# A two-layer graph network on one core: a tile's one-hots as three VectorE broadcasts, self weights copied by POOL, room and landing told in larger groups

## What is computed

```python
# layer 0
agg = segment_sum(h[src], dst, 12500)
z = (1 + eps_gin) * h + agg
z = relu(z @ W1 + b1) @ W2 + b2
z = (z - mean(z, 0)) * rsqrt(var(z, 0) + 1e-5) * gamma + beta
x1 = layernorm(x + (z + x))
# layer 1
support = segment_sum(edge_weight[:, None] * x1[dst], src, 12500)
out = layernorm(x1 + relu(support @ weight))
```

## Time and profile before

| | us |
|---|---|
| timed, median of 3 | 4,327.98 (4,326.99 to 4,332.28) |
| span of the profiled execution | 5,351.1 |
| busy PE / PE weight loads | 3,721.5 (70%) / 3,045.6 (57%) |
| busy POOL | 3,177.6 (59%) |
| busy DVE | 2,301.2 (43%) |
| busy ACT | 1,495.5 (28%) |

### The profile page before, as it was taken

One profiled execution on the slowest core, in us unless ns is written; L12 is line 12 of the kernel. 1 busy time (PEld: TensorE's weight loads), 2 busy tenths in 40 slices (PEclk: granted clock), 3 DMA queues, 4 the chain that ended last, 5 costly groups with the idle time before them and its releaser, 6 DMA issues.

```text
span 5351.1 us, 79415 instructions
## 1 busy us (share of the span) xinstructions
PE 3721.5 (70%) x16131; PEld 3045.6 (57%) x16132; DVE 2301.2 (43%) x5448; ACT 1495.5 (28%) x4377; POOL 3177.6 (59%) x3352
## 2 busy tenths in 40 slices
PE   2677676667667776767742667777777777777777
PEld 2565555555555655656632556566665666665666
DVE  2545454545555544545563233333333333333333
ACT  2444444445444444444552000000000000000001
POOL 6666655565656665666335666666666666666662
PEclk6887888888887878888855789888888888888898
DMA  4333333333333333333293333333333333333331
GB/s 134 93 97 92 99 90 97 90 97 93 95 93 97 93 97 91 96 97 99 62 298 123 90 94 99 96 101 96 100 101 99 95 100 100 102 97 97 100 100 53
DMA packets 298112, 541.14 MB, mean 101 GB/s; under 512 B 77802, under 2 KB 190302, under 8 KB 297838
## 3 DMA queue, kind: packets, MB, share of 16 engines
q0 software_dynamic: 159424, 434.52, 28.3%
q10 hardware_dynamic: 89348, 67.77, 4.0%
q1 hardware_dynamic: 49066, 36.39, 2.2%
HBM read 489.80 MB, written 46.88 MB: 100 GB/s over the span
## 4 chain that ended last, share of the span: by engine, by line
issue 27%; ACTq 16%; another core or an unknown queue 15%; PE 15%; ACT 12%; DVE 9%; DVEq 4%; DMA 2%; SPq 1%; POOL 0%; PEldq 0%; POOLq 0%
PE ps L1419 10%; ACT ones_sb L1613 7%; DVE work L1096 7%; ACTq L1611 4%; ACTq L1613 2%; DVEq L1096 2%; PE ps L1221 2%; ACT ring L1611 2%; ACTq L1642 1%; PE ps L1459 1%; ACT ones_sb L1619 1%; ACTq L1617 1%; ACTq L377 1%; PE ps L1292 1%
## 5 line engine op out<-in xcount | busy, mean ns | idle before, releaser
L548 POOL DMA_INDIRECT ring<-in_x,idx x1664 | 1587.9, 954 | 1039.5 <-issue 456.4
L606 POOL DMA_INDIRECT ring<-x_dram,idx x1612 | 1528.0, 948 | 904.9 <-issue 479.8
L1419 PE MATMUL ps<-ring,work 128*128 x6448 | 1631.3, 411 | 581.1 <-DVE work L1096 387.5
L1419 PEld LDWEIGHTS ps<-ring,work 128*128 128x128 f32 x6448 | 1327.7, 208 | 851.0 <-issue 649.4
L1221 PE MATMUL ps<-ring,ones_sb 128*128 x3708 | 1115.7, 449 | 454.8 <-ACT ones_sb L1619 301.9
L1096 DVE TENSOR_SCALAR work<-ps,dstT,wT 128x256 f32<-128x256 f32 x1612 | 748.0, 536 | 1551.6 <-remote 977.0
L1221 PEld LDWEIGHTS ps<-ring,ones_sb 128*128 128x128 f32 x3708 | 800.4, 225 | 676.6 <-issue 550.2
L1613 ACT ACTIVATE ones_sb<-tile_nodes,dstT 128x128 f32<-128x128 f32 x1854 | 651.0, 391 | 396.5 <-issue 331.1
L1292 PE MATMUL ps<-work 128*128 128x128 f32 x3384 | 499.2, 301 | 203.6 <-issue 148.1
L1292 PEld LDWEIGHTS ps<-work 128*128 128x128 f32 x3384 | 484.0, 216 | 233.5 <-issue 189.8
L1791 ACT ACTIVATE work<-ps 128x512 f32<-128x512 f32 x49 | 29.3, 597 | 1764.2 <-remote 1111.7
(11 more groups left out here) (240 smaller groups left out, 2299.3 us busy)
## 6 DMA issues: line engine op xcount, KB each, us to landing
ring<-in_x,idx POOLq DMA_INDIRECT x1664
ring<-x_dram,idx POOLq DMA_INDIRECT x1612
z_dram<-z_pair ACTq DMA_DIRECT2D x49, 256.0 KB
ones_sb<-x_dram ACTq DMA_DIRECT2D x49, 256.0 KB
ring<-z_dram SPq DMA_DIRECT2D x24, 512.0 KB, 4.1
ring<-in_x SPq DMA_DIRECT2D x24, 512.0 KB, 5.6
x_dram<-ring ACTq DMA_DIRECT2D x24, 512.0 KB
out<-ones_sb ACTq DMA_DIRECT2D x48, 256.0 KB
```

The lines of the kernel that those rows point to most:

```text
L548: nc.gpsimd.indirect_dma_start(out=ring[:, q, c, :], out_offset=None, in_=x, in_offset=bass.IndirectOffsetOnAxis(ap=idx[:, q, c:c + 1], ax ...
L606: nc.gpsimd.indirect_dma_start(out=ring[:, q, c, :], out_offset=None, in_=x1_dram, in_offset=bass.IndirectOffsetOnAxis(ap=idx[:, q, c:c + ...
L1419: last = nc.tensor.matmul(to[:, t * D:(t + 1) * D], ones_of[:, b, c, t * P:(t + 1) * P], ring[:, ds((p + b) & (RING - 1), 1), c, :].rearra ...
```

## The change

In the first stage:

- VectorE makes a tile's one-hots, in three instructions for most tiles: one for the shared pair, one for the eight pairs of `heads_of` (16 chunks x 128 nodes, 2,048 elements per partition), one for `last_of`. Each is a scalar_tensor_tensor whose first input is the chunks' targets from `dstT`, each read 128 times, whose second is `minus_iota` (128 columns) read for every chunk, with the tile's base as scalar: (-target + base) is equal to -column. A tile with 10 pairs or more has a further instruction per two pairs. It always makes all ten, also where fewer are used.
- They stand by hand in VectorE's step: the odd tile's between two halves of `keyed`, the next even tile's after `take`. Each waits until the tile two before is summed (`s_acc`).
- ScalarE keeps only its copies out of PSUM and its DMA issues, in a new order (`two_tiles`).
- The self weights are copied by POOL, 8 pairs at once, after these pairs' gathers. SP loads them for the next round into `self_next` beside the indices.
- POOL waits for room before every fourth pair; SP waits for and tells eight pairs, and also waits for POOL's copy.
- TensorE waits once for a tile's one-hots and twice for its landing.
- The table of tiles is of 16 bits, with other columns.

In the second stage VectorE makes the first four pairs of a bucket's loop after a wait for the head of the bucket before alone.

```diff
-        s_gathered = [sem(f"s_gathered{g}") for g in range(RING // TWO)]
+        s_gathered = [sem(f"s_gathered{g}") for g in range(4)]
+        s_selfed = sem("s_selfed")
...
-                        for g in range(RING // TWO):
-                            sp.wait_ge(s_gathered[g], r * (32 * TWO) + 32 * TWO)
-                            sp.sem_inc(s_landed, TWO)
-                            if (g + 1) * TWO % HALF == 0:
-                                h = g * TWO // HALF
+                        for g in range(4):
+                            sp.wait_ge(s_gathered[g], r * (32 * QUARTER) + 32 * QUARTER)
+                            stand(sp)
+                            sp.wait_ge(s_selfed, r * 4 + g + 1)
+                            sp.sem_inc(s_landed, QUARTER)
+                            if g % 2 == 1:
+                                h = g // 2
                                 sp.dma_start(idx[:, h * HALF:(h + 1) * HALF, :],
                                              srcT[:, ds((i + 1) * RING + h * HALF, HALF), :]).then_inc(s_idx[h], 16)
+                                sp.dma_start(self_next[:, h * HALF:(h + 1) * HALF, :],
+                                             selfT[:, ds((i + 1) * RING + h * HALF, HALF), :]).then_inc(s_idx[h], 16)
...
+            def selves_of(q, of):
+                nc.gpsimd.tensor_copy(ring_self[:, q:q + QUARTER, :], of[:, q:q + QUARTER, :]).then_inc(s_selfed, 1)
+
+            pool.wait_ge(s_selves, 1)
+            for q in range(0, RING, QUARTER):
+                selves_of(q, selfT)
...
-                        if q % TWO == 0:
+                        if q % FOUR == 0:
 
-                            pool.wait_ge(s_entered, r * RING + (q - RING + 3))
+                            pool.wait_ge(s_entered, r * RING + (q - RING + FOUR + 1))
                             stand(pool)
                         for c in range(2):
                             gather(q, c)
+                        if (q + 1) % QUARTER == 0:
+                            selves_of(q + 1 - QUARTER, self_next)
...
+            def ones_of_tile(j, bank):
+
+                new, head, m4, m2, _, _, _, shared, off, sweep = entry(dve, j)
+                counted = sweep * RING + off
+                base = tile_base[:, j:j + 1] if isinstance(j, int) else tile_base[:, ds(j, 1)]
+
+                def equal(to, at, n):
+                    at = nc.s_assert_within(at, 0, ROWS - n, skip_runtime_bounds_check_because=IN_RANGE)
+                    return nc.vector.scalar_tensor_tensor(
+                        out=to.rearrange("p b c n -> p (b c) n"),
+                        in0=dstT[:, ds(at, n), :].rearrange("p b c -> p (b c)").unsqueeze(2).to_broadcast([P, 2 * n, P]),
+                        scalar=base, in1=minus_iota[:, :].unsqueeze(1).to_broadcast([P, 2 * n, P]), op0=ALU.add, op1=ALU.is_equal)
+
+                if not (isinstance(j, int) and j < 2):
+                    dve.wait_ge(s_acc, j - 1)
+                    stand(dve)
+                equal(shared_of[bank], shared, 1).then_inc(s_onehot, 1)
...
+                equal(heads_of[bank], head, BATCH)
+                equal(last_of[bank], m2, 1).then_inc(s_onehot, TILE_ONES - 1)
...
                 members(k)
                 if old >= 1:
-                    keyed(k - 1)
+                    keyed(k - 1, range(PARTS // 2))
+                ones_of_tile(2 * k + 1, 1)
+                if old >= 1:
+                    keyed(k - 1, range(PARTS // 2, PARTS))
                 if old >= 5:
                     z_stats(k - 5)
                 places(k, fore)
                 take(k)
-
+                ones_of_tile(2 * k + 2, 0)
...
                 with dve.If(new < m4):
-                    with dve.Fori(new, m4, 2 * TWO) as p:
+                    dve.wait_ge(s_added2, prev_head + RING)
+                    stand(dve)
+                    for b in range(0, 2 * TWO, TWO):
+                        weighted(loop2[:, b:b + TWO], new + b, TWO)
...
-            def ones_of_tile(j, bank, between=None):
...
+            def two_tiles(k, old, sorts=True, loads=True):
+
+                if old >= 3:
+                    z_out(k - 3)
+                if sorts:
+                    ranks_out(k)
+                summed(k, 0)
+                if loads:
+                    load_x(k + 1)
+                if old >= 2:
+                    hidden_out(k - 2)
                 if old >= 1:
-                    if sorts:
-                        ranks_out(k - 1)
-                    summed(k - 1, 0)
-                if old >= 4:
-                    z_out(k - 4)
+                    turned(k - 1)
+                summed(k, 1)
+                if old >= 1 and (not isinstance(k, int) or k <= NS):
+                    keep_runs(k - 1)
+                    stage(k - 1)
```

More of the change, by code:

```diff
@@ L859, in take, with keyed @@
                 stand(dve)
[L861 to L863 removed]
+            def keyed(k, parts):
+                for q in parts:
                     mine = slice(q * WIDTH, (q + 1) * WIDTH)
@@ L1089, in steps2 @@
             def steps2(j):
-                new, m4, head, m2, end = entry2(dve, j)
+                new, m4, head, m2, end, prev_head = entry2(dve, j)
                 def weighted(to, p, n):
@@ L1100, in steps2 @@
                 with dve.If(new < m4):
-                    with dve.Fori(new, m4, 2 * TWO) as p:
+                    dve.wait_ge(s_added2, prev_head + RING)
+                    stand(dve)
+                    for b in range(0, 2 * TWO, TWO):
+                        weighted(loop2[:, b:b + TWO], new + b, TWO)
+                with dve.If(new + 2 * TWO < m4):
+                    with dve.Fori(new + 2 * TWO, m4, 2 * TWO) as p:
                         for b in range(0, 2 * TWO, TWO):
@@ L1206, in sum_tile @@
             def sum_tile(j, bank, others):
-                new, head, m4, m2, end, off, _, rep, _, _ = entry(pe, j)
+                new, head, m4, m2, end, low, rep, _, off, sweep = entry(pe, j)
+                first = sweep * RING
+                counted = first + off
                 if not (isinstance(j, int) and j < 2):
@@ L1212, in sum_tile, with add @@
                 wide = acc_wide[bank]
[L1213 to L1218 removed]
+                nc.tensor.matmul(wide, zeros[0:1, 0:P], zeros[0:1, 0:D + 1], start=True, stop=False).then_inc(s_added, TILE_ONES)
+                def add(p, ones_of, n):
                     for b in range(n):
@@ L1222, in add @@
                                                     start=False, stop=False)
-                            if is_new and b == n - 1 and c == 0:
+                            if b == n - 1 and c == 0:
                                 last.then_inc(s_entered, n)
-                    last.then_inc(s_added, n)
+                    return last
                 with pe.If(rep > 0):
-                    add(new - 1, shared_of[bank], 1, False)
+                    pe.wait_ge(s_onehot, new + counted + 1)
+                    for c in range(2):
+                        nc.tensor.matmul(wide, shared_of[bank][:, 0, c, :], summands[:, ds((new + (RING - 1)) & (RING - 1), 1), c, :].rearrange("p a d -> p (a d)"),
+                                         start=False, stop=False)
                 with pe.If(new < m4):
@@ L1408, in sum_bucket @@
             def sum_bucket(j, bank, others):
-                new, m4, head, m2, end = entry2(pe, j)
+                new, m4, head, m2, end, _ = entry2(pe, j)
                 to = acc2[bank]
```

210 lines of the change are left out of this document (78 added, 132 removed).

## The result

The kernel after takes 4,477.4 us (4,475.4 to 4,481.5, four runs) against 4,327.5 us (4,325.6 to 4,332.3, four runs) before: a ratio of 1.0345 with a 95% interval of 1.033 to 1.0359, 150 us slower. The profiled run took 4,476.3 us, its span is 4,473.0, so here the profile and the timed runs are the same thing.

What follows compares the result with a forecast made beforehand. The prediction took POOL's gathers to pace the kernel end to end. Hold 144, copies 25, first wrap 9 and last eight pairs 8 made 186 us on 4,328: 4,514 us, range 4,360 to 4,600 (0.82).

Steps and rivals of the forecast that it cites:

- POOL paces the kernel: Whole kernel before: POOL's gathers set the time end to end; their floor sum is 4,338 us against the median 4,328.
- 12 us of backlog: After each stage's last gather: TensorE's remaining work estimated at 12 us, in place of the profile's 52 and 58 us.
- The reason given for the profile's extra 1,023 us: Profile of before: POOL's waits beyond the 0.30 us between gathers belong to the profiled execution, not to timed runs.
- ScalarE's one-hots at 0: First stage: 1,100 us leave ScalarE but lie beside POOL's 2,087 us, so they are worth nothing.
- The second stage's early one-hots at 0: Second stage, first four pairs of a bucket: shortening a 30.6 us bucket that waits for 41 us of gathers gains 0.
- Hold by the heads instruction, 98 x 1.47 = 144 us: First stage: each tile's 2,048-element VectorE instruction with two SBUF inputs delays a POOL gather 1.47 us; bounds 100 to 190.
- The Trainium skill's rule: SBUF access of VectorE and POOL: whoever starts first locks for the whole instruction; would cost POOL 196 us instead of 144.
- Copies, 100 x 0.25 = 25 us: POOL's copies of self weights, 0.25 us each behind a gather: 25 us, bounds 5 and 44.
- First wrap, 9 us: Ring's first wrap: landing is told only after POOL's copies, TensorE does six pairs before POOL continues; 9 us, bounds 0 to 12.
- Last eight pairs, 8 us: First stage's end: last eight pairs told together, leaving TensorE some 8 us more before batch norm; bounds 0 to 15.
- VectorE's cover, "thin, 2 us": First stage: VectorE's 42 us per two-tile block fits under POOL's 44 us, so no direct cost.
- a rival for the whole stage (0.05): First stage: VectorE becomes the pace at 52 us per block, adding 376 us, to about 4,700 us; chance 0.05.

Runs made afterwards that it cites:

- the kernel with ScalarE's load: Kernel before, its tables of entries unsigned 16-bit, with ScalarE's self copy issued twice, the second into a spare place: 4,329.1 us, ratio 1.0.
- the last eight kernels: Later follow-up runs (z statistics earlier, heads instruction cut in four or doubled, repeats) on chips where the kernel before takes some 5,370 to 5,410 us.
- the kernel with everything undone: Changed kernel, one-hots still on VectorE, but minus_iota in PSUM, self copies on ScalarE, no self_next, pairs told by two: 4,331.8 us, ratio 1.0007.
- psum_stats_first: Changed kernel with minus_iota in PSUM and three z statistics taken on VectorE ahead of bucket regions and run targets: 5,410.0 us, ratio 1.0064.

## Why the prediction was right, and where its terms were off

The forecast was 4,514 us, the result 4,477; the range held it.

- **POOL paces the kernel**: right. In after and in the kernel with ScalarE's load POOL sits 0.30 us between gathers and waits for hardly anything else; 156 us of added ScalarE work did nothing. The size of the sum that rests on it, 4,338 us, was met partly by luck: in the kernel with ScalarE's load the end behind the last gather is 30 us and the stretch between the stages 181, where the prediction's 12 us of backlog left 35 and 197, while its two rows of gathers are 7 and 3 us longer than reckoned.
- **The reason given for the profile's extra 1,023 us** was wrong, though the use made of it was right. I called these waits the profiled execution's own. Timed runs of before took 5,356 to 5,442 us beside the last eight kernels, and profiled executions elsewhere agree with their timed runs (4,476.3 and 4,477.4 us in after), so it isn't the recording that differs. One chip took 4,329 us and three others 5,366 to 5,412; whether it is the chip or something else running there no run shows.
- **ScalarE's one-hots at 0**: right, as far as the kernel with everything undone shows it (4,331.8 us beside 4,329.2). The second stage's early one-hots at 0: right, 0.1 us between the two ledgers, though that edit was not run alone.
- **Hold by the heads instruction, 98 x 1.47 = 144 us**: mechanism right, shown by one operand's place; 97 x 1.20 = 116 us measured, 120 with all new instructions. The length was right (2.37 against 2.30), the count too. The step that was off is the mean delay: I spread the gathers evenly over 1.254 us behind a blocking time of 2.1. They aren't spread evenly: 37 of 97 lose 1.13 to 1.18 us because the 256-element instruction before had just let them in, and another 30 lose 0.94 or 0.95. The Trainium skill's rule (SBUF — State Buffer, section "SBUF: two separate sides"), 196 us by my estimate, is further off. Its condition for VectorE, two inputs in SBUF, agrees with the run that puts one of them in PSUM. Its lock for whoever starts first does not agree: no heads instruction grew by a gather's 0.95 us (mean 2,366 ns, longest 2,417, beside a mean of 2,347 without the hold).
- **Copies, 100 x 0.25 = 25 us**: too large. They lie in the 0.30 us between gathers and cost 0.07 us each, 7 us. I had this as the lower bound and took the middle, for want of a row that shows an instruction between two gathers.
- **First wrap, 9 us**: right. The row is

```profile
101.68 0.97 POOL L553 DMA_INDIRECT ring<-in_x,idx  x1 [7.77 <-PE ps L1284]
```

  7.77 us and 0.61 of copies in place of 0.30: 8.1 us; the kernel with ScalarE's load passes this place without a wait. What I left out is that ranks, and with them VectorE's sorting, hang on the same telling: VectorE stands 38.0 us once in after. Held gathers hid that there; with minus_iota in PSUM it stayed to the end of the stage.
- **Last eight pairs, 8 us**: 10.2 us, but for another reason. It is the z statistics behind the regions: TensorE waited 21.9 us for ScalarE's agg, and so had 67 one-hot matmuls, some 17 pairs, left when the last gather ended. It waited for no landing after that.
- **VectorE's cover, "thin, 2 us"**: right, and it mattered more than I said. As long as the hold slowed POOL down it was hidden; with the hold gone it was too thin to make up the late start of the first wrap, and 22 of the 120 us went back. I had it as a rival for the whole stage (0.05), not as what stands at the stage's end.

The measured sum: 120 for the hold, 7 for the copies, 8.1 for the first wrap, 10.2 between the stages, 145 us of the 145.5 between the spans and of the 150 between the medians. The two terms that were too large were so by 24 and 18 us, 42 together, against 37 between forecast and result.

## What to carry to other kernels

Before moving work to an idle engine, ask which engine paces the kernel and what that engine shares with the new place: here 1,100 us came off an engine that nobody waited for, and the new instructions held up, through their two SBUF operands, the one that everybody waits for. One operand in PSUM took nearly all of the hold away; shorter instructions took most of it away on the chips where they were measured. And an engine with little room to spare keeps a late start to the end of the stage: look at what the first round's messages wait for, not only at the steady state. When a profile's span and the timed runs differ, look first whether the busy times fit the timed runs with the waits left out; and at the end of a stage look at the order of the queue of the engine that has lost its lead.

## What the runs showed of the hardware

The chips that took 5,370 us show pauses in which nothing moves. These are the rates in 40 slices of 2.5 us, 3,500 to 3,600 us, in after and in psum_stats_first:

```profile
GB/s 111 103 93 121 100 100 165 268 105 102 105 110 107 102 111 97 105 105 92 115 102 125 93 191 222 120 110 97 103 103 103 110 110 102 108 108 93 111 105 190
```

```profile
GB/s 18 110 100 103 110 103 85 7 105 105 173 223 128 105 0 105 105 105 105 105 105 0 88 103 103 98 110 107 107 108 21 51 234 186 98 93 123 54 8 102
```

On the second, the rate drops to 0 to 21 GB/s in six slices of a hundred microseconds, between them it is much the same, and the gathers of this window (945 ns) and VectorE's weighted one-hots (536 ns, 539 in after) have their usual length. The profile of before has such holes in this window too (15, 0 and 7 GB/s in three slices). The mean granted clock is lower on these chips as well, 0.82 against 0.90 in the kernel with minus_iota in PSUM. What stops the transfers no run here shows, nor how much of the time is the clock's.

A gather takes POOL 0.95 us and 0.30 us more to the next; a 16-element copy put between the two adds 0.07 us; and a gather that VectorE holds ends 0.82 us after the VectorE instruction, whatever that instruction's length (2.37, 0.75 and 0.61 us seen).
